# Last ten batches of an expert stage cut into 128-row tiles: batch layout of a vision-transformer tower with two-of-eight experts

## What is computed

```
flat = layernorm(h).reshape(-1, 192)
probs = softmax(flat @ router_w.T); top_w, top_i = top_k(probs, 2); top_w /= top_w.sum(-1)
for e in range(8):
    w_e = sum(top_w * (top_i == e), -1)[:, None]
    out += w_e * (gelu(flat @ w1[e] + b1[e]) @ w2[e] + b2[e])
h = h + out
```

## Time and profile before

| what | value |
|---|---|
| three runs | 1569.53, 1570.63, 1570.84 us |
| the profiled execution | 1581.96 us, its span 1580.2 us |
| attention stage | 0 to about 861.5 us of the span |
| expert stage | about 861.5 to 1580.2 us |
| granted TensorE clock, mean of the span | 0.961 |

### The profile page before, as it was taken

How to read it: one execution, slowest core, us unless ns; L and a number is a source line. 1 busy time by engine, 2 the same in 40 slices (tenths; PEclk the granted TensorE clock), 3 DMA queues, 4 the chain that set the end, 5 groups by cost and what they waited for, 6 DMA issues and landing times. The chain is left out here.

```text
span 1580.2 us, 50913 instructions
## 1 busy us (share of the span) xinstructions
PE 1426.5 (90%) x17688; PEld 1190.1 (75%) x17689; DVE 1109.0 (70%) x2883; ACT 648.6 (41%) x1136; POOL 896.5 (57%) x900
## 2 busy tenths in 40 slices
PE   5899999999999999999652999999999999999995
PEld 4788888888888788888541677777777777777774
DVE  2577887777878878787444677767777677776763
ACT  2455545554555455544320333333333333333331
POOL 4236656665666556665443356655666656666565
PEclk9999999999999999999755999999999999999998
DMA  5565655656575656554323454444444544444432
GB/s 171 174 184 156 188 160 163 198 146 203 164 200 154 188 160 197 141 163 132 85 63 116 78 63 64 70 65 61 61 64 63 69 63 61 62 63 70 65 46 30
DMA packets 295283, 182.63 MB, mean 116 GB/s; under 512 B 200825, under 2 KB 280901, under 8 KB 294109
## 3 DMA queue, kind: packets, MB, share of 16 engines
q1 hardware_dynamic: 230954, 111.47, 29.0%
q0 software_dynamic: 41680, 41.84, 16.9%
q10 hardware_dynamic: 22499, 27.28, 5.4%
HBM read 83.40 MB, written 65.29 MB: 94 GB/s over the span
## 5 line engine op out<-in xcount | busy, mean ns | idle before, releaser
L993 POOL DMA_INDIRECT out<-y,token x219 | 408.8, 1866 | 77.6 <-issue 77.6
L1007 ACT ACTIVATE act_out<-up,bias 128x384 f32<-128x384 f32 x438 | 253.8, 580 | 429.5 <-PE up L1069 417.2
L1081 PE MATMUL down<-w_hi,g_hi 128*128 x1314 | 323.3, 246 | 4.0 <-issue 2.0
L1083 PE MATMUL down<-w_hi,g_lo 128*128 x1314 | 323.1, 246 | 0.0
L1082 PE MATMUL down<-w_lo,g_hi 128*128 x1314 | 323.1, 246 | 0.0
L1069 PE MATMUL up<-e_xT,w_hi 128*128 128x384 f16 x1314 | 287.8, 328 | 28.4 <-DMA e_xT<-sorted_scratch 25.7
L391 POOL DMA_INDIRECT sorted_scratch<-payload,place x212 | 220.8, 1041 | 59.8 <-issue 56.8
L779 PE MATMUL near<-we,patches 128*120 128x192 f32 x1272 | 223.9, 333 | 18.8 <-DMA patches<-in_xt 11.0
L779 PEld LDWEIGHTS near<-we,patches 128*120 128x120 f32 x1272 | 208.1, 185 | 29.3 <-issue 28.0
L1069 PE MATMUL up<-e_xT,w_lo 128*128 128x384 f16 x876 | 215.7, 328 | 0.0
L1039 DVE TENSOR_TENSOR g_lo<-act_out,g_hi 128x768 f16<-128x768 f32 x219 | 209.9, 959 | 7.6
(11 more groups left out here) (152 smaller groups left out, 2557.4 us busy)
## 6 DMA issues: line engine op xcount, KB each, us to landing
patches<-in_xt SPq DMA_DIRECT2D x53, 720.0 KB
v_diag<-v_scratch SPq DMA_DIRECT2D x159, 89.2 KB
v_scratch<-v_rows SPq DMA_DIRECT2D x53, 191.2 KB, 3.3
tab<-tab_scratch SPq DMA_DIRECT2D x53, 180.0 KB
out<-h ACTq DMA_DIRECT2D x52, 180.0 KB
stage<-in_w ACTq DMA_DIRECT2D x8, 1152.0 KB
k_diag<-qk SPq DMA_DIRECT2D x424, 15.8 KB
stage<-in_w ACTq DMA_DIRECT2D x8, 576.0 KB
```

The lines of the kernel that those rows point to most:

```text
L993: pool.indirect_dma_start(out=out, out_offset=bass.IndirectOffsetOnAxis(ap=token[k][:, n:n + 1], axis=0), in_=y[k % 2][:, n, :], in_offset ...
L1007: act.activation(act_out[:, m, :], up[(MF * k + m) % UPS][:], ACT.Gelu, bias=bias[k % 2][:, m:m + 1], scale=1.0 / WS)\
L1081: pe.matmul(dst, g_hi[k % 2][:, m, cols], high, start=(m == 0), stop=False)
L1083: ins = pe.matmul(dst, g_lo[k % 2][:, m, cols], high, start=False, stop=(m == MF - 1))
```

## The change

The region of an expert is padded to 128 rows only, and the rows are dealt out in two kinds of batches:

- `WHOLE` = ceil((25216 - 8 x 383) / 384) = 58 batches of 384 rows of one expert. That is the number that any split of the pairs is sure to fill.
- All that is left of every expert fits in `TILES` = (25216 + 8 x 127) // 128 - 3 x 58 = 30 tiles of 128 rows. Three tiles, which can be of three experts, make a **mixed** batch; there are 10. `BATCHES` becomes 68.

In a mixed batch every operation that depends on the expert is done for each tile: 3 loads of each kind, 90 matmuls of 128 columns for 30 of 384 in the up product, 18 activations of 128 columns for 6 of 384, ten small VectorE instructions for four, three register reads for one. A token can now be in a batch twice, in two tiles, and so each scatter of a mixed batch after the first waits until the one before has landed. Mixed batches are written out behind the loop. The loop has 13 turns, behind 4 batches.

At the end of the attention stage there are 11 zeroed pieces of `out` and 7 spare tiles (18 DMAs ahead of the wait for the ends, for 2), eight fillings of 128 rows from device memory for eight of 384 from SBUF, and 51 table steps for 28, with tables of 58x8 and 30x9 elements for 73x8. One load of the filler into SBUF goes.

```diff
-REGION = TOKENS + BATCH
+REGION = TOKENS + 128
-BATCHES = (CHOSEN * TOKENS + EXPERTS * (BATCH - 1)) // BATCH
-HEAD = (BATCHES - 2) % 4
+WHOLE = -(-(CHOSEN * TOKENS - EXPERTS * (BATCH - 1)) // BATCH)
+TILES = (CHOSEN * TOKENS + EXPERTS * 127) // 128 - PARTS * WHOLE
+SPARES = TILES - (CHOSEN * TOKENS // 128 - PARTS * WHOLE)
+BATCHES = WHOLE + -(-TILES // PARTS)
+DUMMIES = 128 * (EXPERTS + PARTS)
+HEAD = (WHOLE - 2) % 4
...
             sp.wait_ge(s["zero_mem"], 3)
-            sp.dma_start(out[TOKENS:TOKENS + BATCH, :].rearrange("(p r) c -> p (r c)", r=PARTS), zero_rows).then_inc(s["filled"], 16)
-            sp.wait_ge(s["later_in"], 64)
-            sp.dma_start(sorted_dram[SPARE:SPARE + BATCH, :].rearrange("(p r) c -> p r c", r=PARTS), fill_rows).then_inc(s["filled"], 16)
+            for n in range(DUMMIES // 128):
+                sp.dma_start(out[TOKENS + 128 * n:TOKENS + 128 * n + 128, :], zero_rows).then_inc(s["filled"], 16)
+            for n in range(SPARES):
+                at = 128 * (EXPERTS + n % PARTS)
+                sp.dma_start(sorted_dram[SPARE + 128 * n:SPARE + 128 * n + 128, :], fill[at:at + 128, :]).then_inc(s["filled"], 16)
             sp.wait_ge(s["end_set"], 1)
             for e in range(EXPERTS):
                 at = sp.value_load(end_i[0:1, e:e + 1], min_val=e * REGION, max_val=e * REGION + TOKENS)
-                sp.dma_start(sorted_dram[bass.ds(at, BATCH), :].rearrange("(p r) c -> p r c", r=PARTS), fill_rows)\
-                  .then_inc(s["filled"], 16)
+                sp.dma_start(sorted_dram[bass.ds(at, 128), :], fill[128 * e:128 * e + 128, :]).then_inc(s["filled"], 16)
...
-    with eng.Fori(0, (BATCHES - 2 - HEAD) // 4) as p:
+    with eng.Fori(0, (WHOLE - 2 - HEAD) // 4) as p:
...
-    for u in range(BATCHES - 2, BATCHES):
+    for u in range(WHOLE - 2, BATCHES):
...
             def load(u, k):
+                if mixed(u):
+                    for n in range(PARTS):
+                        tile = PARTS * (u - WHOLE) + n
+                        row = sp.value_load(tile_row[0:1, tile:tile + 1], min_val=0, max_val=SPARE + 128 * (SPARES - 1))
+                        sp.dma_start(xT[k][:, :, tile_cols(n)], sorted_dram[bass.ds(row, 128), 0:NUMBER_AT].bitcast(F16), transpose=True)\
+                          .then_inc(s_xT[k], 16)
+                        sp.dma_start(rows[k][:, n, :], sorted_dram[bass.ds(row, 128), NUMBER_AT:PAYLOAD]).then_inc(s_rows[k], 16)
+                    return
...
                 for n in range(PARTS):
+                    if mixed(u) and n > 0:
+
+                        pool.wait_ge(s_sent[k % 2], SENT * (u // 2) + 16 * n)
                     pool.indirect_dma_start(out=out, out_offset=bass.IndirectOffsetOnAxis(ap=token[k][:, n:n + 1], axis=0),
...
-                    act.activation(act_out[:, m, :], up[(MF * k + m) % UPS][:], ACT.Gelu, bias=bias[k % 2][:, m:m + 1], scale=1.0 / WS)\
-                       .then_inc(s["gelu_done"], 1)
+                    for n in range(PARTS if mixed(u) else 1):
+                        cols = tile_cols(n) if mixed(u) else slice(0, BATCH)
+                        ins = act.activation(act_out[:, m, cols], up[(MF * k + m) % UPS][:, cols], ACT.Gelu, bias=bias[k % 2][:, n, m:m + 1],
+                                             scale=1.0 / WS)
+                    ins.then_inc(s["gelu_done"], 1)
...
+                for n in range(PARTS if mixed(u) else 1):
+                    e, tiles = experts[n], slice(n, n + 1) if mixed(u) else slice(0, PARTS)
+                    dve.tensor_scalar(bias[k % 2][:, n, :], b1s[:, bass.ds(e, 1), :].rearrange("p a m -> p (a m)"), 0.0, None, ALU.add)
+                    dve.tensor_scalar(bias2[k][:, n, :], b2s[:, bass.ds(e, 1), :].rearrange("p a d -> p (a d)"), WS, None, ALU.mult)
+                    dve.tensor_scalar(weight[k][:, tiles], weights[:, tiles, bass.ds(e, 1)].rearrange("p n a -> p (n a)"), 0.0, None, ALU.add)
...
-                    for j, (c, w, h) in enumerate(PRODUCTS):
-                        ins = pe.matmul(up[(MF * k + m) % UPS][:], w1s[h][:, bass.ds(e, 1), w, 128 * m:128 * m + 128].rearrange("p a c -> p (a c)"),
-                                        xT[k][:, c, :], start=(j == 0), stop=(j == len(PRODUCTS) - 1))
+                    for n in range(PARTS if mixed(u) else 1):
+                        cols = tile_cols(n) if mixed(u) else slice(0, BATCH)
+                        for j, (c, w, h) in enumerate(PRODUCTS):
+                            weights = w1s[h][:, bass.ds(experts[n], 1), w, 128 * m:128 * m + 128].rearrange("p a c -> p (a c)")
+                            ins = pe.matmul(up[(MF * k + m) % UPS][:, cols], weights, xT[k][:, c, cols], start=(j == 0), stop=(j == len(PRODUCTS) - 1))
                     ins.then_inc(s["up_done"], 1)
```

More of the change, by code:

```diff
@@ L737, in _ @@
             then(dve.tensor_scalar(count_i, count_i, THIRD_SHIFT, None, ALU.logical_shift_right))
-            then(dve.tensor_copy(count, count_i))
-            then(dve.memset(ends[:, 0:1], 0.0))
-            for e in range(EXPERTS):
-                then(dve.tensor_tensor(ends[:, e + 1:e + 2], ends[:, e:e + 1], count[:, e:e + 1], ALU.add))
-            then(dve.scalar_tensor_tensor(out=first, in0=ends[:, 0:EXPERTS], scalar=-float(BATCH), in1=base, op0=ALU.mult, op1=ALU.add))
-            then(dve.tensor_scalar(first, first, -float(SPARE), None, ALU.add))
+            then(dve.tensor_copy(whole[:, 0:EXPERTS], count_i))
@@ L745, in _ @@
+            count_up(ends, whole)
+            then(dve.scalar_tensor_tensor(out=first[:, 0:EXPERTS], in0=ends[:, 0:EXPERTS], scalar=-float(BATCH), in1=here, op0=ALU.mult, op1=ALU.add))
+            steps_of(first, EXPERTS)
             each = number.unsqueeze(2).to_broadcast(MAP)
             then(dve.tensor_tensor(begun, each, ends[:, 0:EXPERTS].unsqueeze(1).to_broadcast(MAP), ALU.is_ge))
-            then(dve.tensor_tensor(passed, each, ends[:, 1:EXPERTS + 1].unsqueeze(1).to_broadcast(MAP), ALU.is_ge))
@@ new lines, in _ @@
+            then(dve.scalar_tensor_tensor(out=batch_row[:], in0=number, scalar=float(BATCH), in1=whole_sum, op0=ALU.mult, op1=ALU.add))
+            then(dve.tensor_scalar(used[:, 0:EXPERTS], ends[:, 0:EXPERTS], -1.0, float(WHOLE), ALU.mult, ALU.add))
+            then(dve.tensor_scalar(used[:, 0:EXPERTS], used[:, 0:EXPERTS], 0.0, None, ALU.max))
+            then(dve.tensor_tensor(whole[:, 0:EXPERTS], whole[:, 0:EXPERTS], used[:, 0:EXPERTS], ALU.min))
+            then(dve.tensor_scalar(count_i, count[:, 0:EXPERTS], 127.0, None, ALU.add))
@@ new lines, in _ @@
+            then(dve.tensor_scalar(count_i, count_i, 7, None, ALU.logical_shift_right))
+            then(dve.tensor_copy(parts[:, 0:EXPERTS], count_i))
+            then(dve.scalar_tensor_tensor(out=parts[:, 0:EXPERTS], in0=whole[:, 0:EXPERTS], scalar=-float(PARTS), in1=parts[:, 0:EXPERTS],
+                                          op0=ALU.mult, op1=ALU.add))
+            count_up(tile_ends, parts)
+            then(dve.scalar_tensor_tensor(out=tile_first[:, 0:EXPERTS], in0=whole[:, 0:EXPERTS], scalar=float(BATCH), in1=here, op0=ALU.mult, op1=ALU.add))
@@ new lines, in _ @@
+            then(dve.tensor_copy(tile_first[:, EXPERTS:], base[:, EXPERTS:]))
+            then(dve.scalar_tensor_tensor(out=tile_first, in0=tile_ends, scalar=-128.0, in1=tile_first, op0=ALU.mult, op1=ALU.add))
+            steps_of(tile_first, EXPERTS + 1)
+            each = number[:, 0:TILES].unsqueeze(2).to_broadcast(TILE_MAP)
+            then(dve.tensor_tensor(tile_begun, each, tile_ends.unsqueeze(1).to_broadcast(TILE_MAP), ALU.is_ge))
+            then(dve.tensor_reduce(part_sum, tile_begun[:, :, 1:EXPERTS], AX.X, ALU.add))
@@ L1055, in body @@
                 dst = y[k % 2][:]
-                dve.tensor_tensor(dst, down[:, :, 0:D], bias2[k][:].unsqueeze(1).to_broadcast(wide), ALU.add).then_inc(s["biased"], 1)
+                of_tile = bias2[k][:] if mixed(u) else bias2[k][:, 0, :].unsqueeze(1).to_broadcast(wide)
+                dve.tensor_tensor(dst, down[:, :, 0:D], of_tile, ALU.add).then_inc(s["biased"], 1)
                 dve.wait_ge(s["biased"], u + 1)
@@ L1146, in lay_out @@
         "above": np.triu(np.ones((128, 128), f), 1),
[L1147 removed]
+        "numbers": np.arange(WHOLE, dtype=f)[None],
         "token_no": np.concatenate([ROWS * n + np.arange(ROWS, dtype=f)[:, None] for n in range(4)], 1),
```

131 lines of the change are left out of this document (72 added, 59 removed).

## The result

The changed kernel takes 1644.78 us (median of four runs, 1639.84 to 1647.04), the kernel before 1570.74 us beside it (four runs, 1569.53 to 1572.52). The ratio is 1.046, 95% interval 1.044 to 1.049. I had predicted 1559.5 us and a range up to 1577.

What follows compares the result with a forecast made beforehand. TensorE bounds the kernel before; GpSimd was to take over for the last ten batches at 13.0 us each. With -3.5, +0.3 and +0.5 us ahead of them, the end moved -11.1 us: 1570.63 to 1559.5 us, range 1546 to 1577.

Steps and rivals of the forecast that it cites:

- the one headed TensorE: Mixed batches' up product: 90 matmuls take 5.0 us, at most 7.4; TensorE needs 9.5 to 11.9 us a batch.
- under P: P is GpSimd's period for one mixed batch, 13.0 us, ends 11.3 and 13.9; TensorE's time was to stay below it.
- The scatters' wait: GpSimd in mixed batches: each scatter awaits the landing before it, three landings of 2.1 us; this term was to decide.
- rival 4: TensorE's clock falls in its idle gaps of mixed batches, hidden by 3.3 us of slack; chance of a slower result 0.03.
- VectorE, ScalarE, SyncE: Mixed batch: VectorE some 7.4 us, +0.5 us once; ScalarE's activations 5.4 us, SyncE's three loads 8.4 us, both hidden.
- Between the stages: Between attention and expert stages: fillings 8 us, tables 12.5 us and last to end; -3.5 us, bounds -4 and 0.
- Rival 1: Scatter landings are longer under load, slower than before; with 2.77 us landings 1581.5 us; chance 0.17.
- Rival 2: The scatters' wait costs little and TensorE stays the bound over 68 batches: -48 us, 1523 us; chance 0.04.
- Rival 3: Up matmuls go at the upper bound, 0.083 us each, 5 us more ahead of batch 58: 1564.5 us; chance 0.10.
- The range: Whole kernel: P from 11.6 to 14.6 us holds eight in ten, 1546 to 1577 us.
- My own mark: Mixed batches: the prediction would be wrong if carriers stood 9.5 to 10 us apart, or above 14.

Runs made afterwards that it cites:

- Experiment 1: Changed kernel with fixed weight addresses in the up product of mixed batches, register reads kept: 1562.35 us, one run.
- experiment 3: Changed kernel with fixed addresses in both products of mixed batches and no register reads on TensorE there: 1565.27 us, one run.
- experiment 4: Changed kernel with only the first tile of each mixed batch scattered, without the waits between scatters: 1632.35 us, one run.
- Experiment 2: Changed kernel with the down product of mixed batches reusing the up product's expert numbers, three register reads for six: 1623.14 us, one run.
- experiments 1 to 7: Seven kernels, each the changed kernel with one edit, one run each: 1562.35 to 1632.35 us.
- spread kernel: Kernel of experiment 8 with mixed batches at places 8, 14, ... 62 and all batches written out without the loop: 1579.56 us, 1.0026 of the kernel before.
- experiment 5: Changed kernel with TensorE reading one expert number a mixed batch and using it for all three tiles: 1567.58 us, one run.
- experiment 7: Changed kernel with the up product of mixed batches in 60 matmuls, of 256 and 128 columns, for 90 of 128: 1600.29 us, one run.
- experiment 8: Changed kernel with VectorE copying mixed batches' up weights to a fixed tile, read there by TensorE: 1576.45 us, ratio 1.0015 to the kernel before.

## Why the prediction was wrong

The step that failed is the one headed TensorE: "90 x 0.056 = 5.0 us", with 0.083 as upper bound. It measured 0.124 us (0.132 in the mean, 11.9 us for the up product) and, with reads and clock, 20.7 us a batch for the "9.5 to 11.9" on which "under P" rested. The row that I took the earlier trace rows has the right width but fixed addresses; I chose it by shape and never asked what else an instruction needs. What would have told me was in the same trace, the queue's row of L1069 shown above: 46 ns a matmul, on an engine for which three times as many were being asked. My two ends were both matmuls without that cost in sight: 0.056 has no operation, and the down product, whose 0.083 us the change left as it was, has two queue operations (46 and 32 ns) for three matmuls, three tiles' experts or one.

I had weighed a page there. The Trainium skill, TensorE: Matmul & The Clock Gate, Back-to-back issue gap, gives 81 ns for a sustained stream of 128 columns. Experiment 1 sustains 0.056 us through the 90 matmuls of a batch (1480.77 to 1485.79 us), each with its own weights, so this trace does not agree with it. By the page's figure the estimate would still have been near 1564 us.

Point by point:

- **The scatters' wait** ("P = 13.0 us", "GpSimd takes over as the bound"): size right, place wrong. The wait between two scatters is mostly 2.2 to 2.3 us and 2.4 in the mean of twelve (28.6 / 12), for my 2.4 (landing and start), the instruction 1.67 in the mean of eighteen for 1.81; experiment 3 gives 12.3 us a batch. But it does not decide; experiment 4 shows that without it the batches are as far apart.
- **Register reads of TensorE:** not among my steps at all. Six for two cost 2.1 + 0.7 us a batch, and behind the longer gap the clock is down, another 1.8 us (6.3 us for the down product against 4.46). Experiment 2 shows the reads' part.
- **Clock** (rival 4: "stays hidden"): it does fall to 0.55 for 3.7 us behind a gap of 2.1 us, the size I gave. My slack was not there to hide it, since TensorE was the bound.
- **VectorE, ScalarE, SyncE:** right. VectorE is busy 7.38 us a batch for my 7.4, ScalarE's 18 activations take 5.29 us for 5.4; three loads occupy SyncE's queue from 1502.43 to 1509.3, 6.9 us for 8.4, and nobody waits for them.
- **Between the stages** ("-3.5 us"): wrong by its sign. The tables took 13.0 us for 12.5, but they were not the last, as I had it: they end at 849.7 us, and the fillings at 851.1. The eight fillings took 12.35 us for "8" (10.0 to 12.5 in the kernels of experiments 1 to 7). From VectorE's first step on the ends to the first load it is 18.7 us before (843.48 to 862.21), 19.8 after (836.69 to 856.48) and 19.8 to 20.1 in the kernels of experiments 1 to 7, so this part grew by about 1 us. The first load came 5.7 us earlier only because that first step did; first loads of kernels with the same code there spread over several us.
- **Rival 1** (landings longer): some are (waits of 3.4 and 3.0 us among twelve); they are not on the path here. **Rival 2** (TensorE stays the bound) came true in name and for the opposite reason. **Rival 3** was the right place and too small: its upper bound should have come from a matmul with a register operation that nothing covers, and where no row shows one, from both queues in series, 0.056 + 0.046 = 0.102 us, already 9.2 us for the up product and, with 4.5 for the down product, more than my 13.0 for GpSimd.
- **The range** rested on GpSimd alone being able to exceed 13 us. My own mark, "wrong if the carriers stood [...] above 14", is what happened.

What stays open: why an operation of 46 ns adds 0.068 us and not 0.046, what else makes up the saving of experiment 2, and why TensorE stands ahead of up products in the spread kernel. No run separated these.

## What to carry to other kernels

When a matmul is cut into narrower ones, count the queue's own instructions with it (register operations, register reads): a pace holds only for rows with the same way of addressing. If the operand comes from a register, write the loops so that one formed address serves several matmuls (three in experiment 5, with four others between), or put the data at a fixed place. And before fewer batches are counted as gain, list each engine's time for the new batch, in order: here two others stood between the old bound and the saving.

## What the runs showed of the hardware

- A register-addressed weight whose address is new for each matmul: 0.124 us a matmul at 128 columns, and 0.128 where 256 and 128 columns alternate (experiment 7); at a fixed address, or one shared by three, 0.056 us at 128 columns (experiments 1 and 5).
- Three register reads occupy TensorE's queue for about 2 us. It stands idle for what the queue was not ahead by: 2.1 us ahead of the down product of the changed kernel, 0.7 ahead of the up product.
- A scatter of 128 rows that must land before the next starts mostly costs 3.7 to 3.9 us (changed kernel); single waits for a landing take up to 4.2 (experiment 8).
- A turn of the loop costs 0.3 to 0.5 us over five engines (kernels with and without it), though no row names it.
